# Two products of a GPS layer in three single passes, with weight remainders taken by GpSimd, and a new order at the ends of an expert loop

## The reference, cut to what matters

```python
xn = ln(x)
h = xn @ W + b                                    # GNN product, 512 x 512
gnn = relu(w0*h + w1*A@h + w2*A@A@h + w3*A@A@A@h) # A: 128 x 128, from the edges
q, k, v = split(xn @ W_qkv)                       # 8 heads of 64
mix = phi(q) @ (phi(k).T @ v) / (phi(q) . sum(phi(k)) + 1e-6)
x = x + gnn + mix @ W_out + b_out                 # output product, 512 x 512
xn = ln(x)
w = top 4 of 16 of softmax(xn @ gate + bias)
x = x + swiglu(xn, sw1, sw2, sw3) + sum over e of w[e] * swiglu(xn, w1[e], w2[e], w3[e])
# swiglu(x, w1, w2, w3) = (silu(x @ w1) * (x @ w2)) @ w3, hidden width 1365
```

## Time and profile before

| | |
|---|---|
| median of three runs | 542.95 us (542.95 to 545.36) |
| the profiled execution | 542.5 us, span 540.8 us |
| TensorE busy | 521.1 us (96% of the span), 2656 instructions |
| VectorE busy | 425.8 us (79%) |
| ScalarE busy | 333.0 us (62%) |
| GpSimd busy | 7.5 us (1%), 32 instructions |
| loaded from HBM | 189.82 MB, 352 GB/s over the span |
| chain that ended last | TensorE 82%, VectorE 9%, DMA 7%, ScalarE 1% |

### The profile page before, as it was taken

How to read it: one execution, slowest core, us unless ns; L and a number is a source line. 1 busy time by engine, 2 the same in 40 slices (tenths; PEclk the granted TensorE clock), 3 DMA queues, 4 the chain that set the end, 5 groups by cost and what they waited for, 6 DMA issues and landing times.

```text
span 540.8 us, 7513 instructions
## 1 busy us (share of the span) xinstructions
PE 521.1 (96%) x2656; PEld 401.6 (74%) x2656; DVE 425.8 (79%) x422; ACT 333.0 (62%) x304; POOL 7.5 (1%) x32
## 2 busy tenths in 40 slices
PE   7999898898999999999999999999999999999997
PEld 3664333355878888888888888888888888888785
DVE  6734510248999989899898999989999899999983
ACT  1102000135778878788777878877787877878760
POOL 2000000001000000000000000000000000000000
PEclk9998999999999999999999999999999999999999
DMA  8999999999989999999999999999999999975560
GB/s 337 421 420 422 421 421 419 422 410 416 399 300 410 364 395 315 356 389 346 393 309 371 363 351 384 330 370 333 385 356 345 363 335 405 328 322 200 221 215 19
DMA packets 36503, 190.37 MB, mean 352 GB/s; under 512 B 4074, under 2 KB 4202, under 8 KB 30851
## 3 DMA queue, kind: packets, MB, share of 16 engines
q1 hardware_dynamic: 36288, 189.96, 91.2%
q10 hardware_dynamic: 194, 0.14, 0.1%
HBM read 189.82 MB, written 0.26 MB: 352 GB/s over the span
## 4 chain that ended last, share of the span: by engine, by line
PE 82%; DVE 9%; DMA 7%; ACT 1%; issue 1%; POOL 0%; DVEq 0%; ACTq 0%; POOLq 0%
PE ps L1422 28%; PE ps L1460 22%; PE ps L1426 14%; DMA w_set<-in_w 5%; DVE s_lo L817 4%; PE ps L1128 4%; PE ps L1444 3%; PE ps L1283 1%; PE ps L1121 1%; PE ps L1188 1%; DMA w_raw<-in_w 1%; DVE s_lo L829 1%; PE ps L1300 1%; PE ps L1192 1%; PE ps L1178 1%; DMA x<-in_x 1%
## 5 line engine op out<-in xcount | busy, mean ns | idle before, releaser
L817 DVE TENSOR_TENSOR s_lo<-w_raw,s_hi 128x1365 fp32r<-128x1365 f32 x136 | 208.8, 1577 | 11.3 <-ACT s_hi L615 11.1
L615 ACT CAST s_hi<-w_raw 128x1365 fp32r<-128x1365 f32 x136 | 180.5, 1338 | 29.4 <-PE ps L1426 16.9
L1422 PE MATMUL ps<-s_hi,xT_hi 128*128 128x512 f32 (+1 forms) x408 | 153.2, 376 | 1.4 <-DVE hT_lo L1015 1.2
L1422 PE MATMUL ps<-s_lo,xT_hi 128*128 128x512 f32 (+1 forms) x408 | 149.1, 368 | 0.0
L829 DVE TENSOR_TENSOR s_lo<-w_raw,s_hi 128x1536 fp32r<-128x1536 f32 x68 | 105.8, 1578 | 2.0 <-ACT s_hi L627 2.0
L1426 PE MATMUL ps<-s_hi,xT_lo 128*128 128x512 f32 (+1 forms) x408 | 106.2, 368 | 0.0
L627 ACT CAST s_hi<-w_raw 128x1536 fp32r<-128x1536 f32 x68 | 91.2, 1344 | 21.6 <-PE ps L1426 18.9
L1422 PEld LDWEIGHTS ps<-s_hi,xT_hi 128*128 128x128 f32 x408 | 76.6, 188 | 18.3 <-DVE hT_lo L1015 1.4
L1422 PEld LDWEIGHTS ps<-s_lo,xT_hi 128*128 128x128 f32 x408 | 76.8, 188 | 12.2
L1426 PEld LDWEIGHTS ps<-s_hi,xT_lo 128*128 128x128 f32 x408 | 72.6, 188 | 5.7
L1460 PE MATMUL ps<-s_hi,hT_hi 128*128 128x512 f32 (+1 forms) x182 | 73.5, 404 | 0.1
(11 more groups left out here) (210 smaller groups left out, 306.0 us busy)
## 6 DMA issues: line engine op xcount, KB each, us to landing
w_raw<-in_w SPq DMA_DIRECT2D x128, 682.5 KB, 6.3
w_raw<-in_w SPq DMA_DIRECT2D x51, 768.0 KB, 6.1
w_set<-in_w SPq DMA_DIRECT2D x32, 1024.0 KB, 26.2
w_raw<-in_w SPq DMA_DIRECT2D x12, 512.0 KB, 6.1
w_raw<-in_sw SPq DMA_DIRECT2D x8, 682.5 KB, 17.5
wk_sb<-in_wk SPq DMA_DIRECT2D x2, 1024.0 KB, 17.0
wq_sb<-in_wq SPq DMA_DIRECT2D x2, 1024.0 KB, 19.0
gcn_sb<-in_gcn_w SPq DMA_DIRECT2D x2, 1024.0 KB, 13.3
```

The costliest lines, as they stand in the source:

```text
L615: a.copy(s_hi[pair][:, 0:F1], raw[:]).then_inc(hi_ready, 1)
L817: v.tensor_tensor(s_lo[pair][:, 0:F1], raw[:], s_hi[pair][:, 0:F1].bitcast(F32), ALU.subtract).then_inc(lo_ready, 1)
L1422: mm(bank(i + c0 // D)[:, 0:even(n)], xT_hi[:, k], w[:, c0:c0 + even(n)], start=(k == 0 and w is hi), stop=False)
```

## The change

**Products.** The GNN and the output product of the second layer are made like the experts': rounded weights and rounded rows, two remainders, three single passes (`split_product`). For each of the two weights ScalarE rounds 128 x 2048 columns into a tile of its own (`split_high`), and GpSimd subtracts it from the raw weights in place (`split_rest`), GNN first. The transposed x gets rounded by ScalarE and its remainder by VectorE before `scale_xT`; the mixed rows are rounded by ScalarE and their remainder takes the place of VectorE's copy. The passes are ordered: rounded rows by rounded weights, row remainders by rounded weights, rounded rows by weight remainders. The first two stand ahead of the attention product, the third behind it.

**Buffers.** The rounded weights lie where two of the six pairs were; the pairs change places, and ScalarE's `hi_w1(0, 2)` and `hi_w2(0, 0)` get other waits; pads are cleared in another grouping; `xsT` moves.

**First experts.** `gated(0)` stands after two of the four `lo_w1(1, k)`; `router()` stands behind `body(1)`; the copy of the experts' `xnT` for the gate moves from VectorE to ScalarE.

**Tail.** The first down product of the next to last expert stands ahead of the last expert's `w2` units on TensorE, and the loads, roundings and remainders follow: `w3` of the next to last expert is loaded ahead of `w2` of the last, and remainders of `h` stand earlier.

**Start.** Three warming matmuls of 128 columns around the first transposes.

```diff
@@ memory
+    split_at = {"gnn": slot_at(3) + 3 * size_w, "out": slot_at(4)}
+    split_hi = {n: place(f"{n}_hi", [P, KT, D], F32R, at_tail + size_w * i) for i, n in enumerate(split_at)}
+    split_lo = {n: place(f"{n}_lo", [P, KT, D], F32R, at) for n, at in split_at.items()}
-    pair_at = [c.at, c.at + size_pair, at_tail, at_tail + size_pair, slot_at(3), slot_at(3) + 2 * size_w]
+    pair_at = [c.at, c.at + size_pair, slot_at(3), slot_at(3) + size_pair, at_tail, at_tail + size_pair]
...
@@ SyncE
             next_w1(NE - 1)
+            next_w3(NE - 2, kind_of(NE - 2))
             next_w2(NE - 1)
-            next_w3(NE - 2, kind_of(NE - 2))
             next_w3(NE - 1, kind_of(NE - 1))
@@ GpSimd
-            clear_pads(range(4))
+            clear_pads(range(2))
+            def split_rest(name):
+                pool.wait_ge(split_hi_ready[name], 1)
+                pg.tensor_tensor(flat(split_lo[name]), flat(split_raw[name]), flat(split_hi[name]).bitcast(F32),
+                                 ALU.subtract).then_inc(split_lo_ready[name], 1)
+            split_rest("gnn")
+            split_rest("out")
+            pool.wait_ge(k_ps, 2)
+            pool.wait_ge(v_ps, 2)
             pool.wait_ge(q_ps, 2)
-            clear_pads(range(4, 5))
-            pool.wait_ge(y_ps, 2)
-            clear_pads(range(5, PAIRS_N))
+            clear_pads(range(2, 4))
+            pool.wait_ge(wout_ps, 2)
+            clear_pads(range(4, PAIRS_N))
@@ ScalarE
+            for b in range(2):
+                a.copy(xT_hi[:, HALF_T[b]], half_tiles(0, b)).then_inc(split_x_hi, 1)
+            def split_high(name, landed):
+                act.wait_ge(*landed)
+                a.copy(flat(split_hi[name]), flat(split_raw[name])).then_inc(split_hi_ready[name], 1)
             exp_k(1)
+            split_high("gnn", (ld_gnn_w, 16))
             copy_v(1)
+            split_high("out", (ld_wout, 16))
             exp_q(1)
             hi_w1(0, 0)
+            act.wait_ge(mixT_ps, 1)
+            a.copy(mixT_hi[:], tiles(0)).then_inc(mixT_hi_ready, 1)
             hi_w1(0, 1)
+            act.wait_ge(k_ps, 2)
+            act.wait_ge(v_ps, 2)
+            act.wait_ge(q_ps, 2)
             hi_w1(0, 2)
             hi_w1(0, 3)
-            act.wait_ge(q_ps, 2)
-            act.wait_ge(k_ps, 2)
+            act.wait_ge(wout_ps, 2)
             hi_w2(0, 0)
-            act.wait_ge(v_ps, 2)
-            act.wait_ge(y_ps, 2)
             hi_w2(0, 1)
...
+            act.wait_ge(x_lo_ready, 2)
+            a.copy(xnT[:].rearrange("p (b t) n -> p b t n", b=2), both_halves(4)).then_inc(xnT_ready, 1)
@@ ScalarE, last expert, as it is after
             for k in range(KT):
                 hi_w1(last, k)
+            hi_w3(last - 1, 0, ALONE)
+            hT_to_hi(last - 1, 0, ALONE)
             hi_w2(last, 0)
+            hT_to_hi(last - 1, 1, ALONE)
             hi_w2(last, 1)
+            hT_to_hi(last - 1, 2, ALONE)
+            silu(last)
...
+            hi_w3(last, 0, ALONE)
+            hi_w3(last, 1, ALONE)
+            last_hT_to_hi(0, 1)
+            hi_w3(last, 2, ALONE)
+            last_hT_to_hi(1, 2)
+            last_hT_to_hi(2, 3)
+            hi_w3(last, 3, ALONE)
@@ VectorE
+            dve.wait_ge(split_x_hi, 2)
+            for b in range(2):
+                last = v.tensor_tensor(xT_lo[:, HALF_T[b]], half_tiles(0, b), xT_hi[:, HALF_T[b]].bitcast(F32), ALU.subtract)
+            last.then_inc(split_x_lo, 1)
             scale_xT()
...
-            v.tensor_copy(mixT[:], tiles(0)).then_inc(mixT_ready, 1)
+            dve.wait_ge(mixT_hi_ready, 1)
+            v.tensor_tensor(mixT_lo[:], tiles(0), mixT_hi[:].bitcast(F32), ALU.subtract).then_inc(mixT_lo_ready, 1)
...
-            v.tensor_copy(xnT[:].rearrange("p (b t) n -> p b t n", b=2), both_halves(4)).then_inc(xnT_ready, 1)
...
-            router()
             def body(e, kind, carries):
                 for k in range(KT):
+                    if k == KT // 2 and isinstance(e, int) and e == 1:
+                        gated(0, kind, carries)
                     lo_w1(e, k)
-                gated(e - 1, kind, carries)
+                if not (isinstance(e, int) and e == 1):
+                    gated(e - 1, kind, carries)
...
             body(1, kind_of(0), 0)
+            router()
@@ VectorE, last expert, as it is after
             gated(last - 1, ALONE, 0)
+            lo_w3(last - 1, 0, ALONE)
+            hT_to_lo(last - 1, 0, ALONE)
             lo_w2(last, 0)
             hT_to_lo(last - 1, 1, ALONE)
             hT_to_lo(last - 1, 2, ALONE)
+            for k in range(1, KT):
+                lo_w2(last, k)
+            lo_w3(last - 1, 1, ALONE)
+            lo_w3(last - 1, 2, ALONE)
+            gated(last, ALONE, 0)
+            lo_w3(last - 1, 3, ALONE)
             lo_w3(last, 0, ALONE)
+            hT_to_lo(last, 0, ALONE)
+            lo_w3(last, 1, ALONE)
+            hT_to_lo(last, 1, ALONE)
+            hT_to_lo(last, 2, ALONE)
+            lo_w3(last, 2, ALONE)
+            lo_w3(last, 3, ALONE)
@@ TensorE
+            def split_product(name, to, rows, rows_lo, done, steps, cols=slice(0, D)):
+                for i in steps:
+                    k = i % KT
+                    if i == 0:
+                        pe.wait_ge(split_hi_ready[name], 1)
+                    if i == KT:
+                        pe.wait_ge(*rows_lo)
+                    if i == 2 * KT:
+                        pe.wait_ge(split_lo_ready[name], 1)
+                    w = split_lo[name] if i >= 2 * KT else split_hi[name]
+                    last = mm(to, rows[i // KT % 2][:, k], w[:, k, cols], start=(i == 0), stop=(i == 3 * KT - 1))
...
-            project_kv(1, y_ps, gnn_w_sb, range(2))
+            split_product("gnn", bank(1), (xT_hi, xT_lo), (split_x_lo, 1), y_ps, range(2 * KT))
             attend(1)
-            project_kv(1, y_ps, gnn_w_sb, range(2, KT))
+            split_product("gnn", bank(1), (xT_hi, xT_lo), (split_x_lo, 1), y_ps, range(2 * KT, 3 * KT))
...
             for b in range(2):
+                split_product("out", wout_halves[b], (mixT_hi, mixT_lo), (mixT_lo_ready, 1), wout_ps, range(3 * KT), HALF[b])
@@ TensorE, last expert
             transpose_h(last_e - 1, 2, ALONE)
+            down(last_e - 1, 0, ALONE)
             for k in range(KT):
                 up_w2(last_e, k)
-            down(last_e - 1, 0, ALONE)
             down(last_e - 1, 1, ALONE)
+            down(last_e - 1, 2, ALONE)
             transpose_h(last_e, 0, ALONE)
-            down(last_e - 1, 2, ALONE)
+            down(last_e - 1, 3, ALONE)
             transpose_h(last_e, 1, ALONE)
-            down(last_e - 1, 3, ALONE)
             transpose_h(last_e, 2, ALONE)
```

More of the change, by code:

```diff
@@ L131, in gps_kernel @@
     at_tail = c.at
+    split_at = {"gnn": slot_at(3) + 3 * size_w, "out": slot_at(4)}
+    split_hi = {n: place(f"{n}_hi", [P, KT, D], F32R, at_tail + size_w * i) for i, n in enumerate(split_at)}
+    split_lo = {n: place(f"{n}_lo", [P, KT, D], F32R, at) for n, at in split_at.items()}
+    split_raw = {"gnn": gnn_w_sb, "out": wout_sb}
     c = Cursor(slot_at(0))
@@ L157, in gps_kernel @@
     rank_ge = d_rank("rank_ge", [P, EG, P])
-    xsT = place("xsT", [P, KT, P], F32, at_xT)
     ident = d("ident", [P, P])
@@ L197, in gps_kernel @@
     at_rank = d.at
+    xsT = place("xsT", [P, KT, P], F32, at_rank)
     rank_t = [d(f"rank_t{i}", [P, E1, E1]) for i in range(2)]
@@ L214, in gps_kernel @@
     mix = neg_k
+    at_mixT = e.at
     ahT = e("ahT", [P, KT, P])
     gcnT = e("gcnT", [P, KT, P])
-    mixT = gcnT
+    mixT_hi = place("mixT_hi", [P, KT, P], F32R, at_mixT)
+    mixT_lo = place("mixT_lo", [P, KT, P], F32R, at_mixT + KT * P * 4)
     y = e("y", [P, D])
@@ L266, in sem, with flat @@
         return nc.alloc_semaphore(name)
+    def flat(t):
+        return t[:].rearrange("p t n -> p (t n)")
     ld_x, ld_small, ld_rows = sem("ld_x"), sem("ld_small"), sem("ld_rows")
@@ L335, in unit_w2 @@
     def unit_w2(e, k):
-        if isinstance(e, int) and e in (0, NE - 1):
-            return unit_w1(e, KT + k)
+        if isinstance(e, int) and e == 0:
+            return unit_w1(0, KT + k)
+        if isinstance(e, int) and e == NE - 1:
+            return unit_w1(e, KT + 1 + k)
         return UNITS * e - KT + 2 * KT + k
     def unit_w3(e, u):
-        if isinstance(e, int) and e >= NE - 2:
-            return UNITS * (NE - 1) - KT + KT * (e - NE + 4) + u
+        if isinstance(e, int) and e == NE - 2:
+            return unit_w1(NE - 1, KT if u == 0 else 2 * KT + u)
+        if isinstance(e, int) and e == NE - 1:
+            return unit_w1(e, 3 * KT + u)
         return UNITS * e + UNITS + u
@@ L694, in _, with last_hT_to_hi @@
                 hi_w1(last, k)
+            hi_w3(last - 1, 0, ALONE)
+            hT_to_hi(last - 1, 0, ALONE)
             hi_w2(last, 0)
+            hT_to_hi(last - 1, 1, ALONE)
             hi_w2(last, 1)
+            hT_to_hi(last - 1, 2, ALONE)
+            silu(last)
```

(32 more changed lines are left out.)

25 lines of the change are left out of this document (7 added, 18 removed).

## The result

The changed kernel takes 545.33 us (median of 12 runs, 543.85 to 546.36), the kernel before beside it 543.64 us (median of 12, 542.56 to 546.13). The ratio is 1.0032, with a 95% interval of 1.0016 to 1.0047: slower by 1.7 us (0.9 to 2.6). A second measurement of the changed kernel, beside the experiments, gave 1.0046 (1.0029 to 1.0063). The profiled execution took 545.35 us with a span of 543.6.

The account below looks back on a forecast made before the run. The prediction took TensorE to bound the 17 experts, so reordering could win only idle time around them. Its terms, +0.87 + 0.63 - 1.44 = +0.06 us, set on the median of 542.95, gave 543.0 us; range 541.2 to 545.7.

Parts of the forecast that it names:

- The likeliest case: Whole kernel: the summed forecast, 543.0 us against a median of 542.95 before; chance 0.55.
- a rival at 546: Before the first expert: TensorE's longer idle stretch (2.5 us for 1.9) halves its clock, +3 us; chance 0.06.
- rivals 2 and 4: Second GpSimd subtraction passes VectorE's add, 547.4 us, chance 0.07; idle before first expert lowers TensorE's clock, 546, chance 0.06.
- +0.87 us: Attention stage: net delay on y and all behind, GpSimd's hold +1.48 less 0.61 from the GNN product.
- The delay by the hold: Attention stage: GpSimd's first subtraction holds VectorE's bias add, so the attention product comes 1.48 us later.
- rival 2: Attention stage: GpSimd's second subtraction passes VectorE's waiting add, holding VectorE 8.8 us; 547.4 us, chance 0.07.
- GNN 0.61 us earlier on y: Attention stage: four late GNN records save 0.81 us, of which VectorE lets 0.61 through to y.
- The output product worth nothing: Second layer: output product shrinks from 3.62 to 2.8 us, but VectorE, its reader, is held until 130.22, so no gain.
- No wait for h: First to second expert: early gating has h ready at 151.05, so TensorE's 1.3 us wait goes.
- +0.63: First experts: TensorE waits 1.9 us at the second hand-over, less 1.3 us won at the first; net +0.63 us.
- -1.44 us: Tail: the new order removes TensorE's waits of 1.16 us and 0.28 us.
- The rival of a stall in the tail: Tail: last loads start 3 to 4.5 us later, leaving a stall worth 1 us; 544.0 us, chance 0.12.

Follow-up runs that it names:

- the two kernels at full clock: Changed kernel with bias add moved, router in the gap, three warming steps: 539.12 us; kernel before with new order, router in the gap, second warming step: 540.51 us.
- all four traces with 2.5 us: Traces with 2.54 to 2.58 us idle before the first expert: changed kernel twice, with bias add moved (543.3 us), with router in the gap (542.2 us).
- the tail alone: Kernel before with only the last expert's new order and the gate's x copy on ScalarE: 540.83 us, ratio 0.9965.
- four traces and not in a fifth: Fall: changed kernel twice, with three warming steps (542.83 us), kernel before with new order only (543.59 us); none: changed kernel with bias add moved (543.3 us).
- these four kernels: Kernel before; it with new order (543.59 us); with new order and router in the gap (541.39 us); with new tail and gate copy on ScalarE (540.83 us).

## Why the prediction was right or wrong

The range of 541.2 to 545.7 held the time of 545.33, and it lies within 0.5% of the time before, the case that had 0.87. But that is in part luck. The likeliest case was no change (543.0 for 542.95), and both intervals exclude it; by the ratio it is 1.7 us off. The upper end of the range was set for a subtraction of 7 us, which did not come, and what filled the range, the clock, was a rival at 546, outside it, with a chance of 0.06. The second measurement, 545.72, lies at its very edge. (The chances of the slower side don't agree either: rivals 2 and 4 have 0.13 together, "slower by more" has 0.10.)

*The attention stage.* +0.87 us was the term, +0.66 is the row of the table. The subtraction takes 4.53 us for the 4.4 taken, and the add was held until 0.5 us behind its end. The delay by the hold, summed at 1.48 us, measured 1.3: the sum let the add take its full 0.69 us behind the subtraction, and it needed 0.5. When the bias landed made no difference to that (9.61 us behind the keys' product here, 9.02 before). The Trainium skill's rule (SBUF — State Buffer, "Who interferes with whom") is borne out from VectorE's side as well, by the row of 2.44 us; so is the figure of its GPSIMD Engine Reference ("Elementwise — side-by-side cycle accounting"), 4497 ns for an add of that size, by the row of 4.53. That the second subtraction would let the waiting add pass first was my reason against rival 2, and so it went: the add ends at about 119.5, and the second subtraction, which is on record from 118.96, lasts 5.02 us with the add ahead of it and 4.59 without.

*The products.* GNN 0.61 us earlier on y: 0.65 at the first expert, from the two kernels at full clock. The output product worth nothing: its second half ends at 129.7, while VectorE is busy until 130.6. Both right.

*First hand-over.* No wait for h: right. I had said nothing of the remainder behind it, where TensorE waits 0.30 us; it costs nothing here, since VectorE is late for the second hand-over in any case. VectorE's idle time ahead of the gating was put at 3.3 us and is 4.50, as the clock's 1.38 us came on top.

*Second hand-over.* The wait was put at 1.9 us, and its row has 1.90 (2.05 when the drain ahead of it is counted in, as the sum did). Net of the first it was put at +0.63, and the table has +1.07. The path is VectorE's, which from the first gating on has no gap but one: 0.27 us are lost because that gating starts 0.28 us behind the last up product for the nothing that I took, and 0.25 at the wait in front of 172.45, between the last short instruction of the ranking and the loop of the later experts. In the kernel before, where the loop follows a long remainder, eight remainders take 12.01 us with no such wait. Some 0.1 us less at the transposes stands against these. The step was right but short.

*What failed* is the step that closed each of these sums: a wait costs its length. The clock was only a rival, with a chance of 0.06, a price of 3 us and in one place of the two, and its argument against was that the clock had stayed full over 1.9 us in one trace. In all four traces with 2.5 us it fell. At the first expert that cost 1.38 us; behind the second hand-over, where I had no such case at all, 1.56. Together they are 2.9 us of the profiled execution, as much as the whole difference of 2.8. In the medians they seem to weigh less, as the fall behind 1.9 us comes and goes.

*The tail.* -1.44 us was the term, and it measured -1.81 in the trace and -1.9 by the tail alone. TensorE's two waits went as summed; what I had left out is that the first record behind a stop costs more than one in a stream (six records took 1.53 us behind the wait at 512.89, 1.24 elsewhere). The rival of a stall in the tail did not come in this trace; the second trace of the changed kernel has a wait of 0.37 us there, for a remainder of h.

So the signs of all places were right. Against the profiled execution the sum missed by the clock, +2.9, with +0.2 for the stop at the second hand-over, +0.4 for the hand-over itself, -0.2 at the start, -0.2 in the attention stage and -0.4 in the tail.

## What to carry to other kernels

Before work is given to GpSimd, list VectorE's instructions with two inputs in SBUF that fall into its time: one cheap add on the path, held for 1.7 us, took more than the products gave, and moving it behind the subtraction won it back. Work is moved along an engine's order only into a place where that engine is idle: moving nothing but the ranking from behind the second expert's body into the idle stretch that the same edit had opened won back 2.1 to 2.8 us. An idle stretch of TensorE like those here, of 1.9 us and more, is priced with the slow clock behind it, or filled. And a wait is not always worth its length: with the tail alone, the time of the wait for the first h took up nearly all of a slow stretch, so taking that wait away gave 1.3 us without the slow clock and nothing with it.

## What the runs showed of the hardware that I had not expected

The clock falls after the wait is over, when the work is in full swing: behind the wait that ends at 180.46 us the first two records of the next product take 0.48 and 0.41 us, and the third 0.60. The same wait of 1.90 us was followed by a fall in four traces and not in a fifth, and the same stretch of 1.92 us by a fall in two traces of four. The program ahead of that stretch is the same in these four kernels, so it is not the order of the work that tells them apart. Nor does a fall need an idle stretch just ahead of it: in the kernel before, the granted clock is 0.64 from 46 to 48 us and 0.50 from 48 to 50, in the first layer, and TensorE's timeline has no gap from 32.22 us on until then. What decides stays open.
